# A gated recurrence between two feed-forward stages: the halves of the tokens, the residual sum and the squares rearranged

## The reference, cut to what matters

```python
xn = _rmsnorm(x, g_sio)
ln_z = -softplus(-_linear(xn, w_ln_z, b_ln_z))
dt = _linear(xn, w_dt, b_dt)
ln_da, ln_o_da = -softplus(-dt), -softplus(dt)
cs = cumsum(ln_o_da, axis=1)
h = exp(cumlogsumexp(ln_z + ln_da - cs) + cs) + exp(cs) * h0
x = x + _linear(h, w_y, b_y) * _silu(_linear(xn, w_yact, b_yact))
xn2 = _rmsnorm(x, g_ffn)
hid = _linear(xn2, w_fc, b_fc) * _silu(_linear(xn2, w_fcact, b_fcact))
return x + _linear(hid, w_out, b_out)
```

## Time and profile before

| | us |
|---|---|
| median of 3 runs | 555.09 (555.05 to 558.54) |
| the profiled execution | 552.32 |
| its span, first to last instruction | 550.3 |
| the stage of `recurrence` in it | about 342 to 383 |
| busy, share of the span | PE 87%, DVE 68%, ACT 41%, POOL 35% |

### The profile page before, as it was taken

The page is one execution under the profiler, slowest core; times in us unless marked ns, Lnnn a source line. Parts: engine busy times, 40 slices in busy tenths (PEclk is TensorE's granted clock), DMA queues, the critical chain, the costliest instruction groups (busy, mean ns, idle before and its releaser), DMA issues. The chain is left out here.

```text
span 550.3 us, 10856 instructions
## 1 busy us (share of the span) xinstructions
PE 478.3 (87%) x3971; PEld 243.8 (44%) x3971; DVE 372.1 (68%) x918; ACT 223.6 (41%) x453; POOL 193.3 (35%) x334
## 2 busy tenths in 40 slices
PE   2899898998988998988648998878999889999995
PEld 1435344443433433333213988335423334466664
DVE  7545775877766868666887475665679784366565
ACT  1411345355564664767100220522416666624221
POOL 7552737665446437048210002840544000000001
PEclk9999999999998999999878999899999999999999
DMA  7221202134544012000704022000331000350700
GB/s 249 67 59 50 60 1 69 51 88 140 180 136 101 12 51 60 4 2 2 305 1 146 11 88 88 1 0 1 85 89 35 27 3 3 95 137 2 229 21 20
DMA packets 27108, 38.05 MB, mean 69 GB/s; under 512 B 3808, under 2 KB 19744, under 8 KB 26672
## 3 DMA queue, kind: packets, MB, share of 16 engines
q1 hardware_dynamic: 27056, 37.36, 22.3%
HBM read 23.91 MB, written 0.59 MB: 45 GB/s over the span
## 5 line engine op out<-in xcount | busy, mean ns | idle before, releaser
L1098 DVE TENSOR_REDUCE nmax<-bank 128x2 f32<-128x512 f32 (+2 forms) x240 | 144.6, 624 | 76.9 <-PE bank L867 34.1
L979 ACT ACTIVATE arena<-bank 128x512 f32<-128x512 f32 (+2 forms) x256 | 131.0, 527 | 122.1 <-PE bank L871 84.3
L867 PE MATMUL bank<-arena 62*128 62x256 bf16 (+2 forms) x512 | 86.4, 258 | 10.9 <-DVE nmax L1098 5.6
L509 PE MATMUL bank<-causal_qk,identb 128*128 128x512 bf16 x270 | 79.9, 400 | 11.0 <-DVE y L1043 5.4
L871 PE MATMUL bank<-arena 64*128 64x256 bf16 (+2 forms) x512 | 85.9, 256 | 2.2 <-ACT arena L979 1.5
L912 PE MATMUL bank<-arena 128*32 128x256 f32 (+4 forms) x1088 | 72.9, 346 | 8.6 <-ACT arena L979 3.1
L867 PEld LDWEIGHTS bank<-arena 62*128 62x128 bf16 x512 | 29.8, 94 | 77.5 <-issue 48.5
L734 POOL TENSOR_SCALAR_AFFINE_SELECT arena<-arena 128x256 f32<-128x256 f32 x64 | 25.7, 409 | 49.3 <-ACT arena L979 48.5
L509 PEld LDWEIGHTS bank<-causal_qk,identb 128*128 128x128 bf16 x270 | 22.5, 101 | 43.6 <-issue 10.8
L871 PEld LDWEIGHTS bank<-arena 64*128 64x128 bf16 x512 | 30.2, 94 | 16.7 <-issue 7.0
L912 PEld LDWEIGHTS bank<-arena 128*32 128x32 f32 x1088 | 21.4, 109 | 34.6 <-issue 18.9
(11 more groups left out here) (318 smaller groups left out, 817.4 us busy)
## 6 DMA issues: line engine op xcount, KB each, us to landing
arena<-arena SPq DMA_DIRECT2D x96, 128.0 KB, 2.4
fcw<-in_fc1T SPq DMA_DIRECT2D x16, 256.0 KB, 3.7
arena<-in_fc2T SPq DMA_DIRECT2D x1, 4096.0 KB, 12.4
arena<-comb_rows SPq DMA_DIRECT2D x16, 256.0 KB, 4.3
fcw<-in_last SPq DMA_DIRECT2D x1, 2304.0 KB, 8.0
arena<-pos_rows SPq DMA_DIRECT2D x16, 128.0 KB, 2.9
arena<-comb_rows SPq DMA_DIRECT2D x16, 128.0 KB, 4.2
w<-in_w SPq DMA_DIRECT2D x1, 1216.0 KB, 6.3
```

Of the source, the lines that this page charges most:

```text
L509: nc.tensor.matmul(bank[:, :], m.identb[:, :], m.causal_qk[:, 0:4, :], start=True, stop=True)
L867: mins = t.matmul(mout[:, i, :], stack_rows(m, nm, h0 + i, 0, MAX_ROWS)[:, qt * P:(qt + 1) * P], stack_rows(m, nm, h0 + i, 1, MAX_ROWS)[:, ...
L979: s.activation(m.prob[h % 8][:, 0:w], score_bank(n, h)[:, 0:w], ACT.Exp).then_inc(exps, 1)
L1098: v.tensor_reduce(m.nmax[n % 2][:, qt, h0:h0 + nh], MX[c % NMX][:, 0:nh * (k1 - k0)].rearrange("p (h k) -> p h k", h=nh), AX.X, ALU.max, n ...
```

## The change

The halves no longer go side by side. PE projects the first half before it transposes the second; the second's output gate projection comes after the first half's `gated_back`. DVE does product, scans, gate and output of half 0, then of half 1. Into a bank (`sums`, B[2] and B[3]) PE first adds the carried rows x3, by a matmul with the identity (`carried`), and then y, by products with the identity instead of transposes; DVE's `added` and `squares` are gone. ACT squares the sums with an accumulator output, four instructions a half; POOL applies the constants ahead of its power; `scaled` reads the sums' bank. `doubled` forms xr (sum plus x3) on DVE and takes the place of the first add in `residual`. The output gate's sigmoid of half 1 stands behind the squares of half 0 in ACT's queue. The units' banks change with `unit_banks`; the third pair waits for `doubled(0)` (`xr_in`).

```diff
--- before.py
+++ after.py
...
@@ -1660,6 +1661,7 @@
         "ffn_mm", "s_in", "hid_in", "out_mm", "var_ready", "rstd_ready", "zf")]
...
+    squared, mean_in, xr_in = sem("squared"), sem("mean_in"), sem("xr_in")
...
@@ -1667,6 +1669,13 @@
...
+    def sums(c):
+
+        return B[2 + c]
+
+    def unit_banks(u):
+        return ((4, 5), (6, 7), (2, 1))[u % 3]
...
@@ -1696,7 +1705,9 @@
         g.memset(m.arena[:, 16384:20480], 0.0).then_inc(zeroed, 1)
         pool.wait_ge(zeroed, 1)
         for c in range(2):
-            pool.wait_ge(ms_ready, c + 1)
+            pool.wait_ge(squared, c + 1)
+            g.tensor_scalar(m.veps[:, tiles(c)], m.veps[:, tiles(c)], 1.0 / D, RMS_EPS, ALU.mult, ALU.add).then_inc(mean_in, 1)
+            pool.wait_ge(mean_in, c + 1)
             power(c, rs_ready, c + 1)
...
@@ -1709,13 +1720,15 @@
         def transposed(c, count):
             pe.wait_ge(xn_ready, count)
             for i in range(4):
-                ins = t.transpose(B[c][:, i * P:(i + 1) * P], xn[:, 4 * c + i, :], m.ident[:, :])
+                ins = t.transpose(B[c if count <= 2 else 0][:, i * P:(i + 1) * P], xn[:, 4 * c + i, :], m.ident[:, :])
             ins.then_inc(tr_mm, 1)
 
-        def projections(c):
-            pe.wait_ge(tr_in, c + 1)
-            for k, name in enumerate(("dt", "lnz", "yact")):
-                t.matmul(B[2 + 3 * c + k][:, :], w128(m, name), xnT[:, cols(c)], start=True, stop=True).then_inc(p_mm, 1)
+        def projection(c, k):
+            t.matmul(B[2 + 3 * c + k][:, :], w128(m, ("dt", "lnz", "yact")[k]), xnT[:, cols(c)], start=True, stop=True).then_inc(p_mm, 1)
+
+        def carried(c):
+            pe.wait_ge(scaled_in, c + 1)
+            t.matmul(sums(c)[:, :], m.ident[:, :], x3[:, tiles(c), :].rearrange("p t d -> p (t d)"), start=True, stop=False, skip_group_check=True)
 
         def mixed(c):
             pe.wait_ge(h_ready, 2 * c + 2)
@@ -1724,16 +1737,17 @@
         def gated_back(c):
             pe.wait_ge(y_in, c + 1)
             for i in range(4):
-                ins = t.transpose(B[c][:, i * P:(i + 1) * P], yT[:, 512 * c + i * P:512 * c + (i + 1) * P], m.ident[:, :])
+                ins = t.matmul(sums(c)[:, i * P:(i + 1) * P], yT[:, 512 * c + i * P:512 * c + (i + 1) * P], m.ident[:, :],
+                               start=False, stop=True, skip_group_check=True)
             ins.then_inc(yt_mm, 1)
 
         def unit(u):
             c, f = divmod(u, FT)
             if u >= 3:
                 pe.wait_ge(hid_in, u - 2)
-            k = 2 + 2 * (u % 3)
-            t.matmul(B[k][:, :], m.w_fc[:, f * P:(f + 1) * P], xnT[:, cols(c)], start=True, stop=True)
-            t.matmul(B[k + 1][:, :], m.w_act[:, f * P:(f + 1) * P], xnT[:, cols(c)], start=True, stop=True).then_inc(ffn_mm, 1)
+            fc, gate = unit_banks(u)
+            t.matmul(B[fc][:, :], m.w_fc[:, f * P:(f + 1) * P], xnT[:, cols(c)], start=True, stop=True)
+            t.matmul(B[gate][:, :], m.w_act[:, f * P:(f + 1) * P], xnT[:, cols(c)], start=True, stop=True).then_inc(ffn_mm, 1)
 
         def product_first():
             pe.wait_ge(hid_in, FT)
@@ -1743,21 +1757,29 @@
                                    m.w_out[:, f, :], start=(f == 0), stop=(f == FT - 1))
             ins.then_inc(out_mm, 1)
 
-        for c in range(2):
-            transposed(c, c + 1)
-        for c in range(2):
-            projections(c)
-        for c in range(2):
-            mixed(c)
-        for c in range(2):
-            gated_back(c)
-        keep_warm(nc, m, B[7], F_GATED)
+        transposed(0, 1)
+        pe.wait_ge(tr_in, 1)
+        for k in range(3):
+            projection(0, k)
+        transposed(1, 2)
+        pe.wait_ge(tr_in, 2)
+        projection(1, 0)
+        projection(1, 1)
+        mixed(0)
+        carried(0)
+        gated_back(0)
+        projection(1, 2)
+        carried(1)
+        mixed(1)
+        keep_warm(nc, m, B[4], F_GATED)
+        gated_back(1)
         pe.wait_ge(m.mlp_loaded, 48)
         transposed(0, 3)
         pe.wait_ge(tr_in, 3)
         unit(0)
         unit(1)
         transposed(1, 4)
+        pe.wait_ge(xr_in, 1)
         unit(2)
         unit(3)
         pe.wait_ge(tr_in, 4)
@@ -1776,30 +1798,46 @@
 
         def turned(c, g, count):
             act.wait_ge(tr_mm, count)
-            s.activation(xnT[:, cols(c)], B[c][:, :], ACT.Copy, scale=col(m, g)).then_inc(tr_in, 1)
-
-        def silu(u):
-            act.wait_ge(ffn_mm, u + 1)
-            if u >= 2:
-                act.wait_ge(hid_in, u - 1)
-            s.activation(sil[u % 2], B[3 + 2 * (u % 3)][:, :], ACT.Silu, bias=col(m, f"act{u % FT}")).then_inc(s_in, 1)
-
-        s.mul(ndt[:, :], col(m, "dt"), -1.0).then_inc(neg, 1)
-        act.wait_ge(neg, 1)
-        s.activation(table[:, :], ndt[:, :], ACT.Sigmoid).then_inc(neg, 1)
-        for c in range(2):
-            turned(c, "g_sio", c + 1)
-        for c in range(2):
+            s.activation(xnT[:, cols(c)], B[c if count <= 2 else 0][:, :], ACT.Copy, scale=col(m, g)).then_inc(tr_in, 1)
+
+        def gates(c):
             act.wait_ge(p_mm, 3 * c + 1)
             s.activation(og[:, cols(c)], B[2 + 3 * c][:, :], ACT.Sigmoid, bias=ndt[:, :], scale=-1.0)
             s.activation(fg[:, cols(c)], B[2 + 3 * c][:, :], ACT.Sigmoid, bias=col(m, "dt"))
             act.wait_ge(p_mm, 3 * c + 2)
             s.activation(zg[:, cols(c)], B[3 + 3 * c][:, :], ACT.Sigmoid, bias=col(m, "lnz")).then_inc(p_in, 1)
+
+        def out_gate(c):
             act.wait_ge(p_mm, 3 * c + 3)
             s.activation(sg[:, cols(c)], B[4 + 3 * c][:, :], ACT.Sigmoid, bias=col(m, "yact")).then_inc(sg_in, 1)
+
+        def squares(c):
+            act.wait_ge(yt_mm, c + 1)
+            for i in range(4):
+                ins = s.activation(sq[c][:, i, :], sums(c)[:, i * P:(i + 1) * P], ACT.Square,
+                                   accum_out=m.veps[:, 4 * c + i:4 * c + i + 1])
+            ins.then_inc(squared, 1)
+
+        def silu(u):
+            act.wait_ge(ffn_mm, u + 1)
+            if u >= 2:
+                act.wait_ge(hid_in, u - 1)
+            s.activation(sil[u % 2], B[unit_banks(u)[1]][:, :], ACT.Silu, bias=col(m, f"act{u % FT}")).then_inc(s_in, 1)
+
+        s.mul(ndt[:, :], col(m, "dt"), -1.0).then_inc(neg, 1)
+        act.wait_ge(neg, 1)
+        s.activation(table[:, :], ndt[:, :], ACT.Sigmoid).then_inc(neg, 1)
+        turned(0, "g_sio", 1)
+        gates(0)
+        out_gate(0)
+        turned(1, "g_sio", 2)
+        gates(1)
+        squares(0)
+        out_gate(1)
         act.wait_ge(neg, 2)
         s.activation(table[:, :], ndt[:, :], ACT.Silu).then_inc(neg, 1)
         turned(0, "g_ffn", 3)
+        squares(1)
         silu(0)
         silu(1)
         turned(1, "g_ffn", 4)
@@ -1815,19 +1853,16 @@
         def by_tile(t):
             return t.rearrange("p (t d) -> p t d", d=D)
 
-        def squares(x, c):
-            link(v.tensor_tensor(sq[c], x[:, tiles(c), :], x[:, tiles(c), :], ALU.mult))
-            link(v.tensor_reduce(m.veps[:, tiles(c)], sq[c], AX.X, ALU.add))
-            v.tensor_scalar(m.veps[:, tiles(c)], m.veps[:, tiles(c)], 1.0 / D, RMS_EPS, ALU.mult, ALU.add).then_inc(ms_ready, 1)
-
-        def scaled(x, c, count):
-            dve.wait_ge(rs_ready, count)
-            v.tensor_tensor(xn[:, tiles(c), :], x[:, tiles(c), :], m.rstd[:, tiles(c)].unsqueeze(2).broadcast_to([P, 4, D]),
+        def scaled(c):
+            dve.wait_ge(rs_ready, c + 1)
+            v.tensor_tensor(xn[:, tiles(c), :], by_tile(sums(c)[:, :]), m.rstd[:, tiles(c)].unsqueeze(2).broadcast_to([P, 4, D]),
                             ALU.mult).then_inc(xn_ready, 1)
 
-        def scans(c):
+        def added_gates(c):
             dve.wait_ge(p_in, c + 1)
             link(v.tensor_tensor(fg[:, cols(c)], fg[:, cols(c)], zg[:, cols(c)], ALU.mult))
+
+        def scans(c):
             for b in range(2 * c, 2 * c + 2):
                 sl = slice(b * SEQ, (b + 1) * SEQ)
                 v.tensor_tensor_scan(h[:, sl], og[:, sl], fg[:, sl], col(m, "h0"), ALU.mult, ALU.add).then_inc(h_ready, 1)
@@ -1842,20 +1877,18 @@
             v.scalar_tensor_tensor(out=yT[:, cols(c)], in0=B[c][:, :], scalar=col(m, "wy"), in1=sg[:, cols(c)],
                                    op0=ALU.add, op1=ALU.mult).then_inc(y_in, 1)
 
-        def added(c):
-            dve.wait_ge(yt_mm, c + 1)
-            dve.wait_ge(scaled_in, c + 1)
-            link(v.tensor_tensor(xr[:, tiles(c), :], by_tile(B[c][:, :]), x3[:, tiles(c), :], ALU.add))
+        def doubled(c):
+            dve.wait_ge(squared, c + 1)
+            link(v.tensor_tensor(xr[:, tiles(c), :], by_tile(sums(c)[:, :]), x3[:, tiles(c), :], ALU.add))
 
         def residual(c):
-            link(v.tensor_tensor(xr[:, tiles(c), :], xr[:, tiles(c), :], x3[:, tiles(c), :], ALU.add))
             link(v.tensor_tensor(xr[:, tiles(c), :], xr[:, tiles(c), :],
```

(25 more changed lines are left out.)

## The result

The changed kernel takes 549.39 us (median of 6, 547.88 to 550.41), the kernel before 555.78 (median of 6, 554.86 to 560.81): ratio 0.9881, 95% interval 0.9847 to 0.9914, 6.4 us less. The forecast was 553.7 in a range of 551.1 to 556.3, so it is missed on the fast side. The profiled execution took 550.41 with a span of 548.7, only 1.9 less than the profiled one of before. Of these 1.9 us, 1.6 lie in the span and 0.3 outside it: an execution's time exceeds its span by some 2.0 us in the kernel before and by 1.7 in the changed one, throughout. The disagreement between profiles and medians, 1.9 against 6.4, is half of this case.

A forecast was written before the change was run, and what follows sets the result against it. DVE was taken to bound the stage's first part, PE's queue the rest; the second half's transposes coming 1.43 us earlier took 1.4 off the shown median of 555.09, giving 553.7, range 551.1 to 556.3.

The forecast's parts named there:

- The bound and the measure: DVE bounds the stage up to the first scaling, then PE's queue; the gain is how much earlier T comes.
- T: Start of the second half's transposes on PE, 366.46 before; forecast 365.03, 1.43 us gained.
- Part 1: Stage opening on PE: first half's projections go ahead, DVE may multiply its gates 1.73 us earlier; second half not earlier.
- Part 2: First half's scans on DVE take turns with POOL's carried rows, done at 350.7 against 350.74: head start of 1.73 spent.
- Part 3: First half overtakes: its y comes earlier, then turning back on PE by eight product passes takes 1.2 us, to 353.9.
- Part 4: Squares on ACT, 1.96 us a half; DVE idles 1.8 before the second gate; first scaling ends 1.84 earlier, unit 0 at 361.08.
- my list of signs of an error: Signs in the trace: scans done at 349, table load beside a square, scaled waiting for POOL, T later than 366.
- Part 5: Second half: its squares on ACT hold T to 365.03 where PE alone allows 364.62, 0.41 lost; 1.43 us gained.
- Rival (d): Granted PE clock: new idle before first-half wy and unit 0 could bring half clock, costing about 1: 554.7; 0.2 with (b).
- (a): No collision of DVE's scans with POOL: scans done at 349.0, 2.8 to 3.5 gained, 551.6 to 552.3; chance 0.25.
- (b): First half's lead used up by ACT and POOL: 0 to 0.5 gained, 554.6 to 555.1; chance 0.2 with the clock rival.
- (c): Table loads on ACT around the squares, 1.28 us each: 2.4 slower, 557.5; chance 0.1.

The follow-up runs named there:

- again_before: The kernel before, unchanged, run once more: 555.14 us, ratio 0.9979 to before.
- warm_first_gap: The kernel before plus seven useless matmuls between the two wy matmuls: 555.04 us, ratio 0.9966 to before.
- order_only: The changed kernel's new order of halves, but with the old sum and squares put back: 551.68 us, ratio 0.9957 to before.
- after_cold: The changed kernel without its keep_warm, the eight useless matmuls: 551.66 us, ratio 0.9935 to before.

## Why the prediction was wrong

**The bound and the measure, right.** DVE bound the first part, unit 0 to the product ran as PE had it (9.14 us before and after from unit 0), and what T gained the next stage gained to the hundredth.

**Part 1, right.** First sigmoid forecast 2.61 behind the first transposes, measured 2.60; the second half not earlier.

**Part 2, right in kind, too dear.** Scans and L1699 held each other, and the head start was eaten. But the scans ended at 7.99, not 8.61: the product was not held at all (0.69), and the two scans lost 1.40, where I had them wait for two whole L1690, 2.0.

**Part 3, right.** The turning back was given 1.2 and took 1.19 to the first square (352.02 to 353.21).

**Part 4, mis-sized.** A square with its read was given 0.49 from the exponentials of rows 9 and took 0.27 (353.21 to 353.48), the later ones 0.25: four in 1.02, not 1.96. The activation reaches its read after 0.17, not 0.27, and the next one follows 0.10 after the read, not 0.22. The exponentials of rows 9 are issued through `link`, a wait from each to the next; that this made them dear is likely but was not tried. DVE's new wait before the gate was therefore 0.98, not 1.8. POOL, which I had hidden by 0.5 us, was then the last to arrive: the scaling waited 0.61 for it. That was on my list of signs of an error.

**Part 5, the sum for the stage.** Scaling at 15.89 instead of 16.74 (0.85), and the squares of the second half no longer hold T, which follows unit 0 by PE's own 3.54 (0.42): together 1.27, the difference between 2.70 and 1.43. This alone would have been 552.4, inside the range. The 0.3 us outside the span were in no term: the sum added the old 2.0 to the new span, and 1.7 was measured.

**The sum, where it failed.** "The median shown is 555.09, 2.8 above that execution; minus 1.4 it is 553.7." I carried the distance between profile and median over to the changed kernel as if it were an offset of the machine. It belonged to the old order, and the profiled execution had little of it: 555.78 against 552.32 before, 549.39 against 550.41 after. The two other traces in which the gap before unit 0 stood open in the old order have the mark 3.1 and 3.7 us later (44.10 and 44.70 against 41.02). Rival (d) looked at the clock from the wrong side: it priced a fall that the new order might bring, at 1 us, and not those that the old order had in other executions. A fall over the units cost 2.1 and 2.7 us from unit 0 to the mark, and the one in the opening 1.0 to 1.2. That the clock fell once in the profiled stage and not a second time was taken for how the kernel runs. That the profiled execution happened to be a good one was bad luck; that nothing in the sum asked why it was 2.8 below its median was not.

**Rivals.** (a), no collision, was out: the scans and L1699 held each other, at some 0.8 us. Its end of the range, 551.6 to 552.3, is near what the stage's 2.70 make of the forecast's own sum, but by cheaper squares and a shorter hold. (b) was out, since its terms were too dear, all but POOL's lateness. (c) was out: no table load stands beside the squares; between the first sigmoid and unit 0 there is only L1838's for Silu, at 354.95, as L1801's before. The chances did not fit each other either: (c) had 0.1 at 557.5, outside the range, and 0.93 was left for within.

**What stays open.** The profile pair gives 2.7 us in the stage and 0.3 outside the span. In again_before the stage is 3.1 longer, so by these traces the two kernels are 6.1 us apart, and 1.3 less where the clock of the changed kernel falls behind the stage, as in two of its three traces. The medians give 6.4, and 5.9 over all executions of both kernels. The kernel before's best-clocked executions (553.8) are 3.7 above the changed kernel's median, where 3.0 are accounted for; the fall in the opening could be the rest, but no trace of such an execution was taken. How often the clock falls is known from few traces: in the units, in two of the three with the old order and the gap open (again_before and warm_first_gap, not before).

## What to carry to other kernels

When the profiled execution is faster than the timed ones by more than a change could gain, ask first what the others lose, and look for PE gaps in front of work that only PE bounds; a handful of useless matmuls there is the cheapest test, and here it gave some 5 us. The gap right in front of such work was worth most (5.0 against 1.9 for the earlier one, by the ratios), and the filling has to end before the work is due. When an engine's queue is rearranged, look at what now stands in front of its latest customers: moving one clearing and one sigmoid took a further 0.9 us off the stage.

## What the runs showed of the hardware

The granted clock fell in front of the units behind idle times of 2.97 us (order_only) and 2.98 (again_before, warm_first_gap), each with 0.78 more after four transposes, and in after_cold with three gaps of 0.78 to 0.92 between short pieces of work. So it isn't one long gap that decides, and in the profile of before gaps of 2.38 and 0.78 led to no fall in the units. From unit 0 to the mark such a fall cost 1.7 to 2.7 us (21.89 to 22.89 instead of 20.19).

An accumulating activation of 128 elements with its read repeats every 0.25 to 0.27 us; the 256-wide ones of rows 9, with a wait between, had 0.59.

A scan on DVE is held by a tensor-tensor on POOL as a tensor-tensor is (2.79 for two instead of 1.39), and POOL is held in turn (2.82 instead of 2.04). The forecast's rule had been shown in the trace for a tensor-tensor alone.
